# Projecting raw rows of x with centred weights: 1/std is applied behind the projection, x also comes laid out by features, and all instruction lists are written anew

## What is computed

```python
mu = mean(x); var = mean((x - mu) ** 2)
xn = (x - mu) * rsqrt(var + eps) * g + b
q, k, v = xn @ Wq + bq, xn @ Wkv + bkv      # 16 heads of 16
q, k = rotary(q, |x|), rotary(k, |x|)       # then a layer norm per head
a = softmax(causal(q k^T / 4)) @ v          # per sequence
x1 = layernorm(x + a @ Wo + bo)
x2 = layernorm(x1 + xattn(x1, ctx))         # 8 heads of 8 over a band of 256 positions, gate by ctx
y  = layernorm(x2 + ffn(x2))                # ternary weights, gated, width 1024
```

## Time and profile before

| | before |
|---|---|
| median of three runs | 856.19 us (854.46 to 863.31) |
| the profiled execution's own time | 854.88 us |
| its span in the profile | 853.2 us |
| PE busy | 776.2 us, 91% |
| DVE busy | 766.6 us, 90% |
| POOL busy | 692.5 us, 81% |
| ACT busy | 681.0 us, 80% |
| 16 DMA engines, mean busy share | 30.2% (queue 1) |

### The profile page before, as it was taken

One profiled execution on the slowest core, in us unless ns is written; L12 is line 12 of the kernel. 1 busy time (PEld: TensorE's weight loads), 2 busy tenths in 40 slices (PEclk: granted clock), 3 DMA queues, 4 the chain that ended last, 5 costly groups with the idle time before them and its releaser, 6 DMA issues.

```text
span 853.2 us, 23669 instructions
## 1 busy us (share of the span) xinstructions
PE 776.2 (91%) x9593; PEld 464.0 (54%) x9665; DVE 766.6 (90%) x1503; ACT 681.0 (80%) x1331; POOL 692.5 (81%) x689
## 2 busy tenths in 40 slices
PE   5788899999999999999999999999999989889884
PEld 3345445555556665556666655556665556555442
DVE  5999997889999999999999999999999998889653
ACT  3367558678889899889888888999899888778864
POOL 5896578888989999999999999999999897465731
PEclk9999999899999999999999999999999999999999
DMA  8100211111333333333333333333333323334333
GB/s 263 39 25 13 58 39 40 27 35 43 70 67 62 70 77 70 76 71 76 76 66 75 67 62 70 76 74 71 67 76 71 70 64 70 70 64 82 64 76 85
DMA packets 125117, 58.00 MB, mean 68 GB/s; under 512 B 93072, under 2 KB 124048, under 8 KB 125008
## 3 DMA queue, kind: packets, MB, share of 16 engines
q1 hardware_dynamic: 125008, 56.49, 30.2%
HBM read 13.98 MB, written 4.19 MB: 21 GB/s over the span
## 4 chain that ended last, share of the span: by engine, by line
PE 69%; DVE 14%; ACT 7%; issue 3%; SPq 3%; POOL 2%; DMA 2%; POOLq 0%; DVEq 0%; ACTq 0%
PE ps L778 9%; PE ps L579 6%; PE ps L856 5%; PE ps L826 5%; PE ps L842 4%; PE ps L747 4%; PE ps L649 4%; PE ps L710 4%; PE ps L589 3%; DVE rowmax L3017 3%; PE ps L617 3%; PE ps L631 2%; PE ps L817 2%; PE ps L678 2%; PE ps L690 2%
## 5 line engine op out<-in xcount | busy, mean ns | idle before, releaser
L3017 DVE TENSOR_REDUCE rowmax<-ps 128x4 f32<-128x768 f32 x256 | 243.2, 950 | 10.1 <-PE ps L710 9.3
L1744 ACT ACTIVATE prob<-ps 128x768 f32<-128x768 f32 x256 | 207.3, 810 | 32.1 <-PE ps L747 31.9
L2508 POOL TENSOR_TENSOR hsum<-hsum,minus_half 128x32 f32<-128x32 f32 x32 | 175.9, 5495 | 11.0 <-DVE hsum L2942 10.9
L2533 POOL TENSOR_SCALAR_AFFINE_SELECT prob<-prob 128x512 f32<-128x512 f32 (+1 forms) x128 | 112.0, 875 | 24.6 <-ACT prob L1744 24.3
L2535 POOL TENSOR_SCALAR_AFFINE_SELECT prob<-prob 128x1024 f32<-128x1024 f32 (+1 forms) x128 | 114.3, 893 | 0.0
L778 PE MATMUL ps<-prob,v_pad 128*32 128x192 f32 x2048 | 97.2, 331 | 0.2 <-POOL prob L2535 0.2
L710 PE MATMUL ps<-k_rows,q_rows 31*128 31x192 f16 x1024 | 86.7, 247 | 9.1 <-DMA k_rows<-qk_lo 4.2
L747 PE MATMUL ps<-q_rows,k_rows 32*128 32x192 f16 x1024 | 86.5, 247 | 5.7 <-ACT prob L1744 5.4
L778 PEld LDWEIGHTS ps<-prob,v_pad 128*32 128x32 f32 x2048 | 60.3, 110 | 30.7 <-issue 17.1
L826 PE MATMUL ps<-wgu,xsplitT 128*128 128x512 bf16 x226 | 59.4, 380 | 12.0 <-ACT v_own L1653 9.1
L856 PE MATMUL ps<-wproj,hT 128*128 128x256 bf16 x512 | 62.5, 276 | 5.7 <-DVE y L3103 4.9
(11 more groups left out here) (162 smaller groups left out, 2025.8 us busy)
## 6 DMA issues: line engine op xcount, KB each, us to landing
v_swap<-v_own SPq DMA_DIRECT2D x64, 68.0 KB, 2.1
xin<-in_x SPq DMA_DIRECT2D x32, 128.0 KB, 2.2
enc<-in_ctx SPq DMA_DIRECT2D x32, 128.0 KB, 2.3
q_rows<-qk_hi SPq DMA_DIRECT2D x64, 64.0 KB, 2.0
k_rows<-qk_hi SPq DMA_DIRECT2D x64, 64.0 KB, 2.1
out<-yout SPq DMA_DIRECT2D x32, 128.0 KB, 2.0
prob<-in_w_guT SPq DMA_DIRECT2D x4, 512.0 KB, 6.4
q_rows<-qk_lo SPq DMA_DIRECT2D x32, 64.0 KB, 2.0
```

Source lines behind the costliest of these rows:

```text
L1744: copy(prob[:, 2 * c:2 * c + 2, :, :].rearrange("p u a b -> p u (a b)"), ps[:, STB:STB + 2, 0:2 * QW], ACT.Exp, scale=float(XD) ** -0.5).t ...
L2508: g.tensor_tensor(hsum[:, t.two, 1, :], hsum[:, t.two, 0, :], minus_half[:, :], ALU.pow).then_inc(S["head_pow3"], 1)
L2533: g.affine_select(out=lead, in_=lead, compare_op=ALU.is_ge, fill=0.0, base=BAND - 64 * kb, pattern=[[0, 8], [1, cut]], channel_multiplier=-1)
L3017: v.tensor_reduce(of_head[:, hq:hq + 2, 2 * row_of(ng):2 * row_of(ng) + 2], ps[:, MXB:MXB + 2, 0:2 * QW].rearrange("p j (a b) -> p j a b", ...
```

## The change

Five edits, and a rewriting.

1. **x by features.** The host adds an array `xT`: for each tile, x transposed, as [128 features, 2 halves, 128 rows]. SP loads 128 KB of it per tile (`do_xtload`) into three buffers; `xin` is loaded as before.
2. **Raw rows are projected.** `do_xn_nb`, `do_xn`, `do_xnT_ps` and `do_xnT` are gone. The projections read `xT`. The mean goes into the weights: once, ahead of tile 0, `mean_weights` (PE) sums each column of the scaled weights and `center_weights` (DVE) subtracts a 256th of it.
3. **1/std behind the projection.** `do_qk` becomes (ps * rstd_x) + bias, and `do_v` an ACT operation with a scale per row. `rstd_x` has four buffers.
4. **Banks.** One user of the shared banks is gone and the others are dealt anew.
5. **Lists.** Fill, loop order, lags and drain of all five engines are new; so are the places of waits.

```diff
-XNT_B, QK_B, V_B, QKT_B, PT0_B, PT1_B, AT_B, WO_B, MAXT_B, TR_B = 5, 7, 5, 7, 5, 6, 6, 5, 6, 6
-HF_B, Z_B, CT_B, GATE0_B, GATE1_B, UP0_B, UP1_B, DOWN_B, S_B, O_B = 7, 7, 5, 5, 7, 6, 7, 5, 5, 6
+QK_B, V_B, QKT_B, PT0_B, PT1_B, AT_B, WO_B, MAXT_B, TR_B, HF_B = 5, 5, 6, 7, 7, 5, 5, 5, 5, 7
+Z_B, CT_B, GATE0_B, GATE1_B, UP0_B, UP1_B, DOWN_B, S_B, O_B, XP_B = 5, 7, 7, 7, 6, 5, 6, 5, 6, 6
...
+            def do_xtload(t):
+                if t.base > 2:
+                    sp.dma_start(xT[:, t.buf, :, :], t_in["xT"][t.base]).then_inc(s_xt[t.buf], 16)
...
             def put_vswap(t):
+                sp.wait_ge(S["v"], t.at(1, 1))
                 do_vswap(t)
...
+            def mean_weights():
+                pe.wait_ge(s_ready, 1)
+                for c in range(2):
+                    mm(ps[:, MXB, 0:DIM], th[:, 0, 0:128], wqkv[:, c, 0:DIM], start=c == 0, stop=c == 1)
+                for c in range(2):
+                    last = mm(ps[:, MXB + 1, :], th[:, 0, 0:128], wqkv[:, c, DIM:], start=c == 0, stop=c == 1)
+                last.then_inc(s_mean, 1)
...
-            def do_xnT_ps(t):
-                for i in range(2):
-                    last = tr(ps[:, XNT_B, 128 * i:128 * i + 128], xn[:, t.two, 128 * i:128 * i + 128], ident[:, :])
-                last.then_inc(S["xnT_ps"], 1)
...
-                    last = mm(ps[:, QK_B, :], xnT[:, t.two, i, :], wqkv[:, i, 0:512], start=i == 0, stop=i == 1)
+                    last = mm(ps[:, QK_B, :], xT[:, t.buf, i, :], wqkv[:, i, 0:512], start=i == 0, stop=i == 1)
...
-            def do_xn(t):
-                copy(xn[:, t.two, :], xin[:, t.x_buf, :], ACT.Identity, bias=nb[:, t.two, 0, :], scale=rstd[:, t.two, 0, :]).then_inc(S["xn"], 1)
...
-            def do_xnT(t):
-                copy(xnT[:, t.two, :, :].rearrange("p a b -> p (a b)"), ps[:, XNT_B, 0:256], ACT.Copy).then_inc(S["xnT"], 1)
...
-                copy(v_own[:, t.buf, :, 0:AD], ps[:, V_B, 0:256].rearrange("p (h d) -> p h d", d=AD), ACT.Copy).then_inc(S["v"], 1)
+                copy(v_own[:, t.buf, :, 0:AD], ps[:, V_B, 0:256].rearrange("p (h d) -> p h d", d=AD), ACT.Identity, scale=rstd_x[:, t.four, :]).then_inc(S["v"], 1)
...
+            def center_weights():
+                dve.wait_ge(s_mean, 1)
+                for c in range(2):
+                    v.scalar_tensor_tensor(wqkv[:, c, 0:DIM], ps[:, MXB, 0:DIM], -1.0 / DIM, wqkv[:, c, 0:DIM], ALU.mult, ALU.add)
+                    last = v.scalar_tensor_tensor(wqkv[:, c, DIM:], ps[:, MXB + 1, :], -1.0 / DIM, wqkv[:, c, DIM:], ALU.mult, ALU.add)
+                last.then_inc(s_ready, 1)
...
-            def do_xn_nb(t):
-                v.scalar_tensor_tensor(nb[:, t.two, 0, :], mv[:, t.two, 0, 0:1], -1.0, rstd[:, t.two, 0, :], ALU.mult, ALU.mult).then_inc(S["xn_nb"], 1)
...
-                v.tensor_tensor(qk[:, t.two, :], ps[:, QK_B, :], qkv_bias[:, 0:512], ALU.add).then_inc(S["qk"], 1)
+                v.scalar_tensor_tensor(qk[:, t.two, :], ps[:, QK_B, :], rstd_x[:, t.four, :], qkv_bias[:, 0:512], ALU.mult, ALU.add).then_inc(S["qk"], 1)
...
+    out["xT"] = out["x"].reshape(TILES, ROWS, 2, 128).transpose(0, 3, 2, 1)
```

2922 lines of the change are left out of this document (1442 added, 1480 removed).

## The result

The changed kernel takes 874.5 us in the median of 4 runs (872.92 to 875.51); the kernel before took 857.77 beside it. The ratio is 1.0169, with an interval from 1.0115 to 1.0224. I had predicted 847 us, 836 to 858. The profiled execution has a span of 870.6 us, against 853.2 before: 17.4 us more. That overstates it: the profiled execution of before is one of its short ones, and in the runs beside the experiments the kernel before took 860.6 to 861.9 us in the median of 22 to 35. Each ratio from here on is to these; against them the changed kernel's 874.5 would be 1.5% more.

The account below looks back on a forecast made before the run. PE and DVE were both taken as full in the loop's step. From 854.9 us, -10.5 for the loop and +1.5 for the start gave 845.9; with 1.3 to the median, 847 us, range 836 to 858.

Parts of the forecast that it names:

- PE's account of the step: -0.37: PE in the loop: removing the two transposes of `xn` takes 0.37 us off the chain, step 22.77 to 22.40.
- ACT's part hidden: ACT in the loop: `xn` and `xnT` go, v's copy gains a scale; net -0.76 to -0.97 us, hidden by idle.
- The wait for v as slack of 0.4: PE in the loop: 0.4 us a step waiting for v's copy to leave its bank; not booked, PE could reach 22.0.
- DVE as the second full engine: DVE in the loop: full like PE; without `xn_nb` and with longer `qk` net -0.19 us, step 22.58 if idle stays.
- The first rival: Loop step: DVE keeps its gaps and only its part counts, step 22.58, time 853 us; chance 0.20.
- 25 steps x -0.42: Loop: step 22.35 instead of 22.77, 0.42 us less in each of 25 steps, -10.5 us in all.
- The start, +1.5: Before tile 0: averaging and centring delay 4.0 us, less 2.5 for ten `xn_nb`; net +1.5, bounds -0.4 and +1.9.
- The fill and the drain otherwise 0: Drain booked as 0, since its work per tile isn't touched, only its order; fill booked nothing beyond the start's term.
- The late copies: SP's queue: q and k copies late for `mx` 0; 0.4 us a step gives 857, 0.7 gives 865; chance 0.12.
- `qk` at 0.74 us: DVE in the loop: a sign to look for, `qk` with its per-row scale lasting 0.74 us.
- ACT's relief: ACT in the loop: `xn` (588 ns) and `xnT` (379 ns) go, net -0.76 to -0.97 us a step.

Follow-up runs that it names:

- b7: Old lists with all edits of the change, two transposes put back on PE where those of `xn` stood: median step 22.90, ratio 1.004 to the kernel before.
- p1: The kernel before with the two transposes of `xn` done twice in the loop: median step +0.22, ratio 1.0072.
- b5: Old lists with all edits of the change, but v's copy without its scale, as before: median step 22.61, ratio 1.0013 to the kernel before.
- b3: Old lists with all edits of the change, `val` 0 moved ahead of `gate` 0 on PE in the loop: ratio 1.0189 to the kernel before.
- b4: The kernel before with `val` 0 moved ahead of `gate` 0 on PE in the loop: ratio 1.0211.
- p2: The kernel before with DVE's `xn_nb` done twice in the loop: median step -0.01, ratio 1.002.
- the old lists: All edits of the change, but with the order, lags and banks of the kernel before: median step 22.70, ratio 0.9996 to the kernel before.
- c1: The changed kernel with 24 more matmuls without use ahead of tile 3's projection: 868.0 us, ratio 1.0078 to the kernel before.
- c3: The changed kernel with c1's matmuls, SP transfers moved behind awaited ones, 18 and 24 useless matmuls in the drain: 864.3 us, ratio 1.0034 to the kernel before.
- a1: The changed kernel with the `xT` load behind the six copies of q and k on SP: 869.4 us, ratio 1.0094 to the kernel before.
- a2: The changed kernel with the `xT` load and v's two swaps behind the six copies on SP: 869.9 us, ratio 1.0115 to the kernel before.

## Why the prediction was wrong

**PE's account of the step: -0.37, taken from one row of the chain.** The mechanism was right and the size wrong. The row holds two prices: 0.22 for the transposes and 0.15 for coming behind a 32-row pair, and the second stays with whoever comes next (b7, p1: 0.20 and 0.22 a step). Without it the median step fell by 0.08, the 0.09 of v's copy counted against it.

**ACT's part hidden, v's copy among it.** Failed. I had seen that PE waits for this copy and named it as the one place where ACT counts, but then charged its 0.09 us more to ACT's slack. b5 shows them in the step in full.

**The wait for v as slack of 0.4.** Failed twice: half of it was a missing record, and the other half isn't slack that PE could spend on other work, as b3 and b4 show. The counts stood on the page of before (226 and 227 of 256) and in the timeline (3 matmuls where 4 belong); I had not compared them.

**DVE as the second full engine.** Failed: p2 shows that 0.25 us more of it cost 0.04 or less. The first rival, with DVE's account alone, would have given a step of 22.58 and is wrong as well.

**25 steps x -0.42.** Measured: -0.01 in the mean with the old lists, +0.05 with the new ones. The new order pays 0.37 us more for `mx` and `st` and 0.27 more for the transposes, and gets back 0.52 elsewhere; the reasons, lost overlap and more expensive places, are read from the traces and not tried. I took for granted that a new order of nearly the same work costs PE the same.

**The start, +1.5.** The first `qk` was predicted at 20.3 and came at 19.4 to 20.5. By tile 8 it cost about 3 us with the old lists and with the new ones, where my bound was 1.9; of the 2.5 us that I booked in exchange for ten `xn_nb` in the fill the old lists show no sign, within their scatter.

**The fill and the drain otherwise 0, "only its order".** This is the step that turned the sign. Fill and drain together became some 16 us longer, 3 of them the start. By the maxima the order took up to 9 or 10 us in the fill beside the 2 of the clock at tile 3, and 4 behind the last maxima; the division is rough, and which places of the order cost them stays open, beyond tile 3 (c1) and the last products (c3). I had compared the lists in the loop, at three places, and not at all where PE is not full, and where a stop can cost twice, by itself and by the clock behind it (3.75 us instead of 1.96 at tile 3).

**The late copies, chance 0.12.** The mechanism is there, at the place I named, in 3 of 18 steps, and worth at most 0.1 us a step in the mean (a1, a2). It isn't what made the kernel slower.

Right were `qk` at 0.74 us, ACT's relief, and the first `qk`; the range missed since it took fill and drain as given.
